# Second attention: a unit of the maxima takes two heads for both query tiles, in place of four heads for one

## The reference

```
x = x + xattn(layernorm(x), ctx)          # 16 heads, 4096 keys
x = x + attn(layernorm(x))                # 16 heads, window of +-32
x = x + ffn(layernorm(x))                 # 16 banks, the 2 best for each token

# attn
q, k, v = split(x @ w_qkv + b_qkv)
scores  = q k^T / sqrt(16) + mask          # mask: 0 where |i - j| <= 32, else -inf
out     = softmax(scores) v
return out @ w_out + b_out
```

## Time and profile before

| | |
|---|---|
| time, median of 3 runs | 1172.65 us (1172.49 to 1173.07) |
| profiled execution, span | 1170.5 us |
| time outside of the span (median minus span) | 2.15 us |
| PE busy | 1145.5 us, 98% of the span |
| DVE busy | 842.1 us, 72% |
| ACT busy | 705.4 us, 60% |
| first unit of the maxima begins | 831.8 us |
| last unit of the maxima ends | 933.5 us |

### The profile page before, as it was taken

How to read it: one execution, slowest core, us unless ns; L and a number is a source line. 1 busy time by engine, 2 the same in 40 slices (tenths; PEclk the granted TensorE clock), 3 DMA queues, 4 the chain that set the end, 5 groups by cost and what they waited for, 6 DMA issues and landing times.

```text
span 1170.5 us, 29569 instructions
## 1 busy us (share of the span) xinstructions
PE 1145.5 (98%) x12054; PEld 707.2 (60%) x12054; DVE 842.1 (72%) x1638; ACT 705.4 (60%) x897; POOL 361.5 (31%) x335
## 2 busy tenths in 40 slices
PE   8989999999999999999999999999999999999998
PEld 5455455566655566655556664444566679878777
DVE  4887899977899987789997779993364683233325
ACT  4437878877788787777887778886433321112111
POOL 3285563113651413353321141021120222222210
PEclk9999999999999999999999999999999998999999
DMA  7676676465475555656555445411130119999993
GB/s 243 106 166 177 161 153 142 127 144 130 119 154 140 119 117 133 158 132 148 122 142 117 106 94 125 75 18 52 21 98 15 27 76 400 405 396 390 402 390 126
DMA packets 64655, 186.28 MB, mean 159 GB/s; under 512 B 20104, under 2 KB 29960, under 8 KB 56584
## 3 DMA queue, kind: packets, MB, share of 16 engines
q1 hardware_dynamic: 60260, 172.70, 53.3%
q0 software_dynamic: 2432, 7.11, 1.9%
q10 hardware_dynamic: 1828, 4.57, 1.1%
HBM read 137.60 MB, written 39.58 MB: 151 GB/s over the span
## 4 chain that ended last, share of the span: by engine, by line
PE 89%; DVE 3%; ACT 3%; DMA 2%; issue 1%; SPq 1%; ACTq 0%; POOL 0%; DVEq 0%; POOLq 0%
PE psum L750 22%; PE psum L732 17%; PE psum L702 11%; PE psum L1163 5%; PE psum L1191 5%; PE psum L600 5%; PE psum L616 4%; PE psum L805 2%; PE psum L1188 2%; PE psum L1157 2%; DVE part_max L1535 1%; ACT wts L1253 1%; PE psum L933 1%; PE psum L799 1%; DMA ctx_in<-in_ctxT 1%
## 5 line engine op out<-in xcount | busy, mean ns | idle before, releaser
L1545 DVE TENSOR_REDUCE part_max<-psum 128x1 f32<-128x512 f32 x952 | 599.6, 686 | 88.8 <-PE psum L702 87.5
L1253 ACT ACTIVATE wts<-psum 128x1024 f32<-128x1024 f32 x512 | 518.8, 1024 | 100.8 <-PE psum L732 99.9
L750 PE MATMUL psum<-wts,vals 128*17 128x256 f32 x4096 | 307.2, 384 | 0.5 <-ACT o_raw L1296 0.5
L732 PEld LDWEIGHTS psum<-queries,keys 51*128 51x128 f32 x2048 | 155.7, 185 | 187.4 <-issue 154.1
L732 PE MATMUL psum<-queries,keys 51*128 51x256 f32 x2048 | 255.2, 326 | 2.2 <-ACT queries L1285 0.2
L702 PE MATMUL psum<-keys,queries 51*128 51x512 f32 x1024 | 218.9, 410 | 4.4 <-DVE part_max L1535 2.8
L750 PEld LDWEIGHTS psum<-wts,vals 128*17 128x17 f32 x4096 | 74.9, 95 | 119.2 <-issue 92.4
L2023 POOL CAST key_high<-key_low 128x1024 fp32r<-128x1024 f32 x28 | 29.1, 1038 | 355.1 <-ACT key_low L1266 355.1
L702 PEld LDWEIGHTS psum<-keys,queries 51*128 51x128 f32 x1024 | 109.7, 185 | 20.0 <-DVE part_max L1535 10.8
L1451 ACT ACTIVATE hid<-psum,b1s 128x128 f32<-128x128 f32 (+1 forms) x124 | 31.7, 351 | 113.2 <-PE psum L1163 76.8
L2025 POOL TENSOR_TENSOR key_low<-key_low,key_high 128x1024 fp32r<-128x1024 f32 x28 | 66.6, 2378 | 2.3
(11 more groups left out here) (278 smaller groups left out, 1377.5 us busy)
## 6 DMA issues: line engine op xcount, KB each, us to landing
w1s<-in_W SPq DMA_DIRECT2D x31, 1024.0 KB
w2s<-in_W SPq DMA_DIRECT2D x31, 1024.0 KB
keys<-k_high SPq DMA_DIRECT2D x232, 128.0 KB, 4.0
keys<-k_low SPq DMA_DIRECT2D x116, 128.0 KB, 4.5
k_high<-key_high SPq DMA_DIRECT2D x28, 512.0 KB, 5.1
k_low<-key_low SPq DMA_DIRECT2D x28, 512.0 KB, 5.4
ctx_in<-in_ctxT SPq DMA_DIRECT2D x12, 768.0 KB, 7.7
ctx_in<-in_ctxT ACTq DMA_DIRECT2D x4, 768.0 KB, 12.9
```

Source lines behind the costliest of these rows:

```text
L732: m = e.matmul(bank(S_BANKS[S_NO["s", n] % 2] + i)[:, hh * SEQ:(hh + 1) * SEQ], keys[64 * i:64 * i + STK, hh, c, at:at + P], queries[g % 3 ...
L750: i = e.matmul(bank(O_BANK)[32 * j:32 * j + VW, 0:SEQ], vals[:, t, h * VW:(h + 1) * VW], wts[n % NW][:, j * SEQ:(j + 1) * SEQ], start=(t = ...
L1253: i = e.activation(wts[n % NW], s_bank(job, 2), ACT.Exp, scale=QSCALE)
L1545: e.reduce_max(part_max[g % 2][:, hq, c:c + 1], bank(M_BANKS[n % 3]), AX_X).then_inc(dve_max, 1)
```

## The change

A unit now takes two heads (2u and 2u+1 for unit u) for both query tiles. Each head has a bank of its own, which holds query tile 0 in columns 0 to 159 and query tile 1 in columns 160 to 319. So the mask goes in as one matmul of 320 columns for each bank, the four fp32 matmuls follow without a wait in their midst, and `pe_even2` is gone. Two matmuls into one bank are always of the same head and so on the same strip. DVE's reduce reads the same 640 columns, and writes its four maxima at [query tile, head] instead of in a row.

```diff
-            def max2(p, qt):
+            def max2(p, u):
 
                 b, g, m, par = heads_of(p)
-                keys_at, tok = b * SEQ + qt * (SEQ - WIN), b * SEQ + qt * P
-                if p == 0 and qt == 0:
+                if p == 0 and u == 0:
                     e.wait_ge(dve_early, 10)
                     e.wait_ge(pool_mask2, 1)
                 else:
-                    e.wait_ge(dve_m2, 2 * p + qt)
-                for odd in range(2):
+                    e.wait_ge(dve_m2, 2 * p + u)
+                for i in range(2):
+                    e.matmul(bank(W_BANKS[i])[:, 0:2 * WIN], identb, wmaskb.rearrange("p t w -> p (t w)"), start=True, stop=False)
+                for qt in range(2):
+                    keys_at, tok = b * SEQ + qt * (SEQ - WIN), b * SEQ + qt * P
                     for i in range(2):
-                        e.matmul(bank(W_BANKS[i])[:, odd * WIN:(odd + 1) * WIN], identb, wmaskb[:, qt],
-                                 start=True, stop=False)
-                    if odd:
-                        e.wait_ge(pe_even2, 2 * p + qt + 1)
-                    for i in range(2):
-                        r = slice(32 * (2 * i + odd), 32 * (2 * i + odd) + 32)
-                        t = e.matmul(bank(W_BANKS[i])[:, odd * WIN:(odd + 1) * WIN], q2[r, par, m, tok:tok + P],
-                                     k2[r, m, keys_at:keys_at + WIN], start=False, stop=True)
-                    t.then_inc((pe_even2, pe_m2)[odd], 1)
+                        r = slice(32 * (2 * u + i), 32 * (2 * u + i) + 32)
+                        t = e.matmul(bank(W_BANKS[i])[:, qt * WIN:(qt + 1) * WIN], q2[r, par, m, tok:tok + P],
+                                     k2[r, m, keys_at:keys_at + WIN], start=False, stop=(qt == 1))
+                t.then_inc(pe_m2, 1)
...
-            def max2(p, qt):
-
-                e.wait_ge(pe_m2, 2 * p + qt + 1)
+            def max2(p, u):
+
+                e.wait_ge(pe_m2, 2 * p + u + 1)
                 src = bank(W_BANKS[0], 2).rearrange("p (b c) -> p b c", b=2)[:, :, 0:2 * WIN]
-                e.tensor_reduce(neg_max2[:, qt].rearrange("p (b h) -> p b h", b=2),
-                                src.rearrange("p b (h w) -> p b h w", h=2), AX_X, ALU.max, negate=True).then_inc(dve_m2, 1)
+                e.tensor_reduce(neg_max2[:, :, 2 * u:2 * u + 2].rearrange("p t h -> p h t"),
+                                src.rearrange("p b (t w) -> p b t w", t=2), AX_X, ALU.max, negate=True).then_inc(dve_m2, 1)
```

More of the change, by code:

```diff
@@ L487, in build @@
             "dve_rows2", "pe_early", "dve_early", "pool_vones2", "pool_neg0", "pool_mask2")
-        pe_half, act_half, dve_half, pe_even2 = semaphores("pe_half", "act_half", "dve_half", "pe_even2")
+        pe_half, act_half, dve_half = semaphores("pe_half", "act_half", "dve_half")
         dve_rows3, st_rows, pe_t3, act_t3, pe_lg, dve_sub, act_prob, dve_both = semaphores(
```

## The result

| | before | after |
|---|---|---|
| median, both on one chip | 1172.49 us (1170.92 to 1173.07) | 1164.65 us (1162.03 to 1166.94), 5 runs |
| ratio | | 0.9918, interval 0.9889 to 0.9947 |
| profiled execution, span | 1170.5 us | 1163.5 us, timed at 1165.31 |
| PE busy | 1145.5 us | 1135.5 us |
| first reduce of the maxima, to the last one | 833.33, 100.33 us later | 833.29, 92.88 us later |

The change makes the kernel faster, by less than one per cent. The ratio on record is 0.9918. It gives 1162.9 on the median beside it (1172.49) and 1163.0 on 1172.65, which is right at the low end of the range (1162.9), and its interval reaches beyond it, from 1159.6 to 1166.4.

The account below looks back on a forecast made before the run. PE's queue was taken to pace the second attention. 9.6 - 0.9 - 0.45 - 0.25 = 8.0 us saved, taking the median from 1172.65 to 1164.6; range 1162.9 to 1167.4, the forecast's own part 1163.5 to 1166 (64%).

Parts of the forecast that it names:

- Columns and rounds: In each unit of the maxima: mask 0.38 us, scores 0.74 to 0.76, saving 0.30; 32 units give 9.6 us.
- The reloads: Score stretch on two strips: weights exchanged three times per strip, taken as hidden; far end all of the 0.18 exposed.
- Exposed reloads: Rival, 4%: in a unit's scores, two more weight loads cost 0.24 of the 0.30; 1170.9, no change.
- neighbouring strips: Rival, 3%: in the scores, heads 0 and 1, then 2 and 3, stream one after the other; 1180.5, slower.
- The removed wait: The wait on `pe_even2` inside a unit: dropping it gives nothing by itself.
- guess: DVE operation ahead of the reduce of (2, 0) waits for a DMA; three units' savings, 0.9 us, are lost.
- Pieces beside POOL: Groups 2 and 6, DVE operations slower while POOL works: 0.25 and 0.20 us of the saving lost.
- The last groups: Groups 14 and 15, reciprocals delay reduces; last unit's saving hidden, most given back next step; 0.25 us lost in all.
- The other groups: Remaining head groups: a late second reduce is covered by scores2 (1.55 us on PE), so cost 0.
- The 2.15 us: Difference between profiled span and median, taken to stay: span 1162.5, median 1164.6.
- from 936 us on the work is the same, and moves forward as a whole: Everything after the second attention: unchanged work, shifted earlier by the full 8 us.
- rival 3: 11%: at the last block's start, the clock rises after the first matmuls, costing 1.7 us; 1166.3.

Follow-up runs that it names:

- the kernel with two stretches of each: Changed kernel with each query tile's mask right ahead of its scores again, two mask and two score stretches per unit; 1175.24 us, ratio 1.0004.

## Why the prediction was right and where it was wrong

**What paces the stage** was right. PE's queue became shorter and the stage with it; DVE's idle time before the reduces fell by 8.8 us, where about 9 was foretold.

**Columns and rounds** were right: mask 0.38 us, scores 0.74, a unit 1.12, so 0.31 saved where 0.30 was taken; 32 x 0.31 = 9.9 for 9.6.

**The reloads** cost nothing: four rounds on two strips in 0.74, three exchanges of weights on each strip in it. Were the two additional loads of 0.184 exposed, the stretch would take 1.11 us. One strip's four loads alone, one after the other, would take 0.74, and all eight of both strips lie within 0.57. By the rule of the Trainium skill ("TensorE: Matmul & The Clock Gate", Part 3, The mechanism) a load to a strip whose matmuls are in flight does not overlap them. Here each strip's loads do, in 0.57 us while its matmuls run, and the measurement decides. *Exposed reloads* and *neighbouring strips* are both out.

**The removed wait** cost nothing, as foretold; the kernel with two stretches of each shows it.

**guess** was right in its mechanism, and the size was off by the issue of the DMAs. The shift of the next reduce fell from 0.97 us behind (1, 1) to 0.06 behind (2, 0); with the 0.31 of the unit in between, 1.22 us were lost, not 0.9. SP's four DMAs begin 4.83 us after the first reduce in the kernel before (838.16) and 4.52 in the changed one (837.81): the unit (0, 1) brought them forward by 0.31, and three units are lost behind them, 0.93, as foretold. The rest is that SP took 3.41 us to issue four DMAs, where it took 3.02 before; 0.09 of this came back, since the reduce began 0.21 behind `guess` in place of 0.30. That SP took longer is no effect of the change: the kernel before's second profile has 3.30 us for the same four,

```profile
838.17 3.30 SPq L2312 DMA_DIRECT2D o_close<-o_raw  x4
```

and the changed kernel's second one 3.25. Splitting the DMAs over two queues gave 1.1 to 1.2 us back.

**Pieces beside POOL**: 0 in group 2 (0.25 taken), 0.33 in group 6 (0.20 taken). **The last groups**: 0.35 for 0.25, and all of it in group 14, where the moved reciprocal took it away. The last unit's saving was hidden in group 15 (0.28), as foretold, and the next step gave all of it back, not most. **The other groups**: nothing, as foretold, by the cover named. In group 11 a late reduce had lost the 0.3 of its unit, and the unit behind had it back.

Sum: 9.9 - 1.2 - 0.35 - 0.35 = 8.0 us, as in the forecast; the errors of the terms took each other away, which is luck. The trace has it: 7.45 between the first and the last reduce, 0.3 of the first unit ahead of that, 0.28 behind it, 8.03 in all. Since this execution had come to the first unit 0.27 later than the kernel before, 7.77 of it are seen at 940 us.

**The 2.15 us** between span and median were too many. They set the span of one execution against the median of three. Wherever time and span of one execution are both on record, 73 times, the time is 1.75 to 1.93 us above the span, so this term put the time 0.3 us too high.

**Two more steps failed.** The first is "from 936 us on the work is the same, and moves forward as a whole". It did not in this execution: 1.56 us were given back by the first matmul of the last block, and 0.82 regained in it, where PE no longer stands still ahead of matmuls that need new weights (0.70 us before). The kernel before takes 194.51, 194.21 and 193.90 us for that block in its three profiles, so the gain in it is not the change's alone. So 7.77 - 1.56 + 0.82 = 7.0, and the span fell to 1163.5 and not to 1162.5. That is rival 3's place and about its price (1.7), but only half its mechanism: the clock was back at its full level when the block began. It was at 0.50 for the 10.2 us before, in place of 6.8, and the product L1113 lay across its fall; 0.61 of the 1.56 us is that product (1.78 against 1.17). The gather's step makes up the rest (7.72 us for its DMA in the chain, 6.76 before). One part of its landing comes 1.3 us behind the others, and why stays open; the clock does not explain it. These are the rows, each from the chain, of the changed kernel:

```profile
961.75 7.72 DMA xin<-rows_x,from_row
```

and of the kernel before, with its product from the timeline:

```profile
965.40 1.17 PE L1116 MATMUL psum<-at_tile,at_row 128*128 128x24 f32 x8 [0.18 <-POOL at_tile L2207]
...
968.91 6.76 DMA xin<-rows_x,from_row
```

The second, and the one that put the result at the edge, is the width of the range. "1163.5 to 1166" and the low end of 1162.9 were put together from the bounds of the terms alone, over a median whose three runs lay within 0.6 us. A term for the measurement was put at nothing, though the prediction itself names 2.3 us as what a measurement of this kernel can tell from no change. With more runs the kernel before goes from 1169.6 to 1180.7 us, once 1185.3, and the changed one from 1162.0 to 1169.4; the spread goes with the granted clock, as shown above. Two comparisons of the same two kernels gave 0.9918 and 0.9939, which is 1163.0 and 1165.5 on the median of 1172.65. These two lie 2.5 us apart; half of that to either side, for the measurement alone, belonged in the range, and would have put its low end at 1161.6.

## What to carry to other kernels

A stretch of small matmuls has a fixed price, here about 0.1 us for a bf16 mask stretch and 0.2 for an fp32 stretch on 32 rows, beside 0.43 ns for each column and pass. So when a queue alternates between two kinds, merging the stretches pays; dropping the semaphore between them by itself did nothing, and here the arithmetic from neighbouring rows foretold it to 0.01 us.

Before counting a saving per unit, look down the other engines' queues for the item that does not hang on the engine made faster: a DMA behind four others (1.2 us) or a long reciprocal between two short operations (0.36 us) swallows what was saved ahead of it, and moving that item is then the next change. The two moves together cost no work and brought the stage down by another 1.5 us.

Three runs that agree within 0.6 us don't measure the scatter of a kernel. A range needs a term for it, and the granted clock of each run should be read beside its time: here 0.001 of it went with about 1 us. A profile of each kernel should be taken more than once before a difference of 1 us outside of the changed stage is given a cause.

## What the runs showed of the hardware that was not expected

- Two strips are enough to hide fp32 weight loads of 184 ns behind rounds of 0.137 us of columns, and it hardly matters whether matmuls of one strip stand next to each other in the queue (0.75 against 0.74 us).
- SP took between 3.02 and 3.60 us to issue the same four DMAs, in different profiles, and what hung on them moved by as much.
- Small DVE operations on 8 columns took up to 0.77 us beside a POOL operation (0.77 and 0.66 in group 6), though not all did; with POOL idle they took 0.17 to 0.20. Which of them meet POOL shifts by tenths of a microsecond: in the profile with heads 0 and 2 paired, one of group 6's four took 0.59 and the others 0.17 to 0.18.
- The level of 1.2 GHz ahead of the last block lasted 3.4, 6.8 or 10.2 us in one piece, in the kernel before as 3.4 and then 6.8, or as 10.2. PE was busy all through each of these stretches; in the changed kernel it had been busy for 1.30 of the 3.20 us just before. A product in the fall took 1.78 us in place of 1.12 to 1.17.
- The time of a run goes with its mean granted clock: in the kernel before 1169.58 to 1173.72 us at 0.991 or above (21 executions), 1175.50 to 1185.27 at 0.988 or below (10).
- The first DMA out of ACT's queue took 1.32 us to issue, beside SP's first ones; on SP the same DMA took 0.60.
